# Layer 1 of the second and third chunk as seven block products, with weights streamed through a ring

## The reference

```python
interaction = jnp.einsum('bnd,bmd->bnm', bottom_output, bottom_output)
interaction_flat = interaction[:, _TRIL_R, _TRIL_C]
x = jnp.concatenate([bottom_mlp_output, interaction_flat, zero_pad], axis=1)
x = jax.nn.relu(x @ W0.T + b0)
x = jax.nn.relu(x @ W1.T + b1)
x = jax.nn.relu(x @ W2.T + b2)
x = jax.nn.relu(x @ W3.T + b3)
return x @ W4.T + b4
```

## Time and profile before

| | us |
|---|---|
| median of three runs (458.95 to 461.52) | 460.08 |
| the profiled execution, its own time | 456.55 |
| its span, first to last instruction | 454.7 |
| TensorE busy in the span | 443.1 |
| chunk two, from one layer 4 to the next (150.2 to 257.2) | 107.0 |
[...]

### The profile page before, as it was taken

One profiled execution on the slowest core, in us unless ns is written; L12 is line 12 of the kernel. 1 busy time (PEld: TensorE's weight loads), 2 busy tenths in 40 slices (PEclk: granted clock), 3 DMA queues, 4 the chain that ended last, 5 costly groups with the idle time before them and its releaser, 6 DMA issues.

```text
span 454.7 us, 12454 instructions
## 1 busy us (share of the span) xinstructions
PE 443.1 (97%) x5623; PEld 372.7 (82%) x5623; DVE 220.4 (48%) x414; ACT 136.9 (30%) x234; POOL 0.7 (0%) x6
## 2 busy tenths in 40 slices
PE   8998899999999999999999999999999999999995
PEld 7997888888888778888888788888788789999973
DVE  4876357343655452422325263324137878656343
ACT  4774333313332222111113222121113654422141
POOL 0000000000000000000000000000000000000000
PEclk9999999999999999999999999999999999999999
DMA  8999668463229325632671224723336120460100
GB/s 306 387 383 408 232 206 305 145 223 151 94 76 401 124 80 192 237 128 94 253 258 81 79 80 149 288 94 127 144 104 192 40 92 11 134 230 6 41 0 0
DMA packets 24102, 74.74 MB, mean 164 GB/s; under 512 B 2930, under 2 KB 9074, under 8 KB 20466
## 3 DMA queue, kind: packets, MB, share of 16 engines
q1 hardware_dynamic: 24050, 73.95, 45.3%
HBM read 65.55 MB, written 8.40 MB: 163 GB/s over the span
## 4 chain that ended last, share of the span: by engine, by line
PE 91%; DVE 4%; issue 2%; ACT 1%; DMA 1%; SPq 0%; DVEq 0%; ACTq 0%
PE work L1061 18%; PE work L1062 17%; PE work L1063 17%; PE acc L1061 8%; PE acc L1062 8%; PE acc L1063 8%; PE gps L1070 7%; PE acc L1088 2%; PE work L1088 1%; PE gps L1063 1%; PE gps L1062 1%; PE gps L1061 1%; DMA xfirst<-x_t 1%; PE gps L1111 1%; DVE turned L758 1%
## 5 line engine op out<-in xcount | busy, mean ns | idle before, releaser
L1061 PE MATMUL work<-h1h,w1s 128*128 128x512 f32 (+1 forms) x208 | 81.4, 391 | 0.0
L1063 PE MATMUL work<-h1l,w1s 128*128 128x512 f32 (+1 forms) x208 | 79.4, 382 | 0.0
L1062 PE MATMUL work<-h1h,w1s 128*128 128x512 f32 (+1 forms) x208 | 79.3, 381 | 0.0
L558 ACT ACTIVATE act_out<-work,bias 128x512 f32<-128x512 f32 (+1 forms) x56 | 36.7, 656 | 106.6 <-PE work L1063 105.0
L1063 PE MATMUL work<-featL,w0h 126*128 126x512 f32 (+5 forms) x160 | 55.4, 347 | 1.9 <-issue 1.9
L1062 PE MATMUL work<-featH,w0h 126*128 126x512 f32 (+5 forms) x160 | 55.9, 349 | 1.4 <-issue 1.4
L1061 PE MATMUL work<-featH,w0l 126*128 126x512 f32 (+5 forms) x160 | 57.1, 357 | 0.0
L1061 PE MATMUL acc<-h2h,w2l 128*128 128x512 f32 x128 | 51.0, 398 | 0.0
L796 DVE CAST h2h<-act_out 128x512 fp32r<-128x512 f32 x32 | 13.6, 426 | 75.7 <-ACT act_out L558 75.6
L1062 PE MATMUL acc<-h2h,w2h 128*128 128x512 f32 x128 | 49.9, 390 | 0.0
L1063 PE MATMUL acc<-h2l,w2h 128*128 128x512 f32 x128 | 49.8, 389 | 0.0
(11 more groups left out here) (127 smaller groups left out, 591.2 us busy)
## 6 DMA issues: line engine op xcount, KB each, us to landing
xraw<-x_t SPq DMA_DIRECT2D x48, 432.0 KB, 6.1
w1s<-w_parts SPq DMA_DIRECT2D x20, 1024.0 KB, 4.9
stage<-w_t SPq DMA_DIRECT2D x16, 512.0 KB, 5.9
w_parts<-w1s SPq DMA_DIRECT2D x8, 1024.0 KB, 4.9
xfirst<-x_t SPq DMA_DIRECT2D x9, 432.0 KB, 6.5
xmid<-x_t SPq DMA_DIRECT2D x5, 432.0 KB, 10.8
w0raw<-w_t SPq DMA_DIRECT2D x4, 512.0 KB, 10.5
w2raw<-w_t SPq DMA_DIRECT2D x4, 512.0 KB, 12.3
```

The costliest lines, as they stand in the source:

```text
L558: act.activation(act_out[:, slot(layer, m, more), cols], bank[:, cols], ACT.Relu, bias=bias[:, row:row + 1]).then_inc(relu_done, 1)
L1061: pe.matmul(dst, wl, ah, start=start, stop=False)
L1062: pe.matmul(dst, wh, ah, start=False, stop=False)
L1063: return pe.matmul(dst, wh, al, start=False, stop=stop)
```

## The change

- Chunks two and three do layer 1 in blocks too, as chunk four does; the gram units, pair picks and transposes for the next chunk are written by hand into the layers: units 0 and 1 behind layer-0 tiles 3 and 5, unit 2i + 2 behind P7 and unit 2i + 3 behind P3 of set i, the transposes of sub-batch i - 1 behind P6 of set i, the last ones ahead of the last layer-2 step. VectorE's picks of sub-batch i stand behind its two splits of set i.
- All S sums and their parts are made in chunk one, from the raw tiles in `stage` (which come in pairs i, 4 + i), and kept in device memory (`s_parts`, `keep_s`). `load_w1` waits for the sums of the pair before.
- Weights of the blocks come through `ring`, one place of 512 KB for each of the seven blocks, refilled when its block is done (`load_block`).
- Blocks and their sums use three banks; P1 and P5 are both copied out by ScalarE, U4 and C22 are made from the copy; C21 now stands ahead of C22, and both splits behind C12. The answers of the chunk before stand behind U2 of the first set.
- Gram units from chunk three's on use one bank, so each waits for the eviction of the one before. x has 4 slots.
- In chunk one layer 1 goes over its tiles in the order 0, 4, 1, 5, ..., and W2's parts follow that order.

```diff
-XSLOTS = 8
+XSLOTS = 4
...
-SUMS = ("U2", "U4", "C11", "U3", "C22", "C21", "C12")
+SUMS = ("U2", "U4", "C11", "U3", "C21", "C22", "C12")
...
+        def place(i, name):
+            banks = gps[:, 1, :], work[:, 0, :], work[:, 1, :]
+            return banks[(NB * i + BLOCKS.index(name)) % 3][:, 0:HALF]
...
+        UNIT_AT = {14: 1, 27: 2, 39: 3, 51: 4, 63: 5, 75: 6, 87: 7}
+        TURN_AT = {34: 0, 55: 1, 79: 2, 99: 3}
...
+        def unit_bank(g, u):
+            return gps[:, u % 2 if g == 1 else 0, :]
+        UNIT_BEHIND = {3: 0, 5: 1}
...
+        W2_AT = {33: 0, 46: 2, 77: 1, 90: 3}
+        W2_ORDER = list(W2_AT.values())
+        S_SUM_AT = {at + n: (i, n) for i, at in enumerate((20, 48, 73, 99)) for n in range(4)}
+        S_LO_AT = {at + 3 * n: (i, n) for i, at in enumerate((26, 54, 80, 105)) for n in range(2)}
...
             def load_w1(m):
                 if m >= 2:
                     sp.wait_ge(w1_done, m - 1)
-                sp.dma_start(stage[:, m % 2, :], w1[m, :, :]).then_inc(w_in[m % 2], 16)
+                    sp.wait_ge(s_sums, m // 2 * 4)
+                sp.dma_start(stage[:, m % 2, :], w1[L0_ORDER[m], :, :]).then_inc(w_in[m % 2], 16)
...
+            def keep_s(i):
+                sp.wait_ge(s_lo, 2 * i + 2)
+                for t, part in enumerate((sh, sl)):
+                    sp.dma_start(s_parts[i, :, :, t, :].rearrange("b p c -> p b c"),
+                                 part[:, i % 2, :, :].bitcast(f32)).then_inc(s_kept, 16)
+            def load_block(c, i, j):
+                    sp.wait_ge(block_done, nth_block(c, i - 1, BLOCKS[j]))
+                elif c > 1:
+                    sp.wait_ge(block_done, nth_block(c - 1, SETS - 1, BLOCKS[j]))
+                if c == 1:
+                    if (i, j) == (0, 0):
+                        sp.wait_ge(tile_done, nth(0, 1, MT1 - 1) + 1)
+                        for kept_slot in w1_kept:
+                            sp.wait_ge(kept_slot, kept(MT1 - 1))
+                        sp.wait_ge(s_sums, 4 * SETS)
+                    sp.wait_ge(s_kept, 32 * (i + 1))
+                name = BLOCKS[j]
+                if name in ("P1", "P2"):
+                    src = w1_parts[i, :, :, 0:WQ] if name == "P1" else w1_parts[i, :, :, WQ:]
+                elif name == "P4":
+                    src = w1_parts[SETS + i, :, :, WQ:]
+                    src = s_parts[i, ("P5", "P6", "P7", "P3").index(name), :, :, :]
+                sp.dma_start(ring[:, j, :, :].bitcast(f32), src).then_inc(ring_in[j], 16)
...
+            def first_body():
+                waits = {0: (2,), 1: (3,), 2: (5,), 3: (6,), 4: (7,), 5: (8,), 6: (9,), 7: ()}
+                stored = {1: 0, 3: 1, 5: 2, 7: 3}
+                for m in range(MT1):
+                    if m == 1:
+                        next_two(0, 3)
+                    if m == 2:
+                        next_two(0, 4)
+                    keep_w1(m)
+                    for u in waits[m] if m != 1 else ():
+                        next_two(0, u)
+                    if m + 2 < MT1:
+                        load_w1(m + 2)
+                    if m in stored:
+                        keep_s(stored[m])
+                load_x0(2)
+                for j in range(NB):
+                    load_block(1, 0, j)
...
+                    next_two(c, 2)
+                    next_two(c, 3)
+                for i in range(SETS):
+                    for j in range(NB):
+                        if i + 1 < SETS:
+                            load_block(c, i + 1, j)
+                        elif more:
+                            load_block(c + 1, 0, j)
+                        units = {(0, 4): 4, (0, 6): 5, (1, 4): 6, (1, 6): 7, (2, 4): 8, (2, 6): 9}
+                        if more and (i, j) in units and (units[(i, j)] < UNITS or later):
+                            next_two(c, units[(i, j)])
+                        if (i, j) == (1, 2):
+                            answer(c - 1)
+                            if later:
+                                load_x0(c + 2)
...
+            def block_out(c, i, name, dst):
+                act.wait_ge(block_done, nth_block(c, i, name))
+                ge(act, sum_done, nth_sum(c, i, name="C22") - NS if name == "P5" else nth_sum(c, i, "C11") - NS)
+                act.activation(dst, place(i, name), ACT.Copy).then_inc(copy_done, 1)
+            def relu_set(c, pos):
...
+            def layers(c, more):
+                for m in range(EARLY, MT0):
+                    relu(c, 0, m, work[:, m % 2, :])
+                    if m % 2 == 0:
+                        t1_hi_part(c, m // 2)
+                    elif m < MT0 - 1:
+                        others_hi_part(c, m // 2)
+                    if more and m in UNIT_BEHIND:
+                        grams_from_psum(c + 1, UNIT_BEHIND[m])
+                for i in range(SETS):
+                    block_out(c, i, "P1", P1_OUT)
+                    block_out(c, i, "P5", P5_OUT)
+                    if more and i:
+                        pairs_hi_part(c + 1, i - 1)
+                    if more and i < SETS - 1:
+                        grams_from_psum(c + 1, 2 * i + 2)
+                    relu_set(c, 2 * i)
+                    relu_set(c, 2 * i + 1)
+                    if more and i < SETS - 1:
+                        grams_from_psum(c + 1, 2 * i + 3)
+                if more:
+                    pairs_hi_part(c + 1, SETS - 1)
...
+                dst, block, part = {"U2": (U23, "P6", P1_OUT), "U4": (U4, None, P5_OUT), "C11": (first[:, left], "P2", P1_OUT),
+                                    "U3": (U23, "P7", U23), "C21": (second[:, left], "P4", U23),
+                                    "C22": (second[:, right], None, P5_OUT), "C12": (first[:, right], "P3", U4)}[name]
+                if block:
+                    dve.wait_ge(block_done, nth_block(c, i, block))
+                    dve.wait_ge(copy_done, 2 * (SETS * (c - 1) + i) + 2)
+                ge(dve, sum_done, nth_sum(c, i, name) - 1)
+                dve.tensor_tensor(dst, place(i, block) if block else U23, part, ALU.add).then_inc(sum_done, 1)
...
+            def layers(c, more):
+                for k in range(1, KQ):
+                    first_of_two(c, k)
+                    second_of_two(c, k)
+                for i in range(SETS):
+                    set_sum(c, i, "U2")
+                    if i == 0:
+                        answers(c - 1)
+                    set_sum(c, i, "U4")
+                    set_sum(c, i, "C11")
+                    if more and i:
+                        pairs_lo_part(c + 1, i - 1)
+                    set_sum(c, i, "U3")
+                    set_sum(c, i, "C21")
+                    set_sum(c, i, "C22")
+                    set_sum(c, i, "C12")
+                    split(c, 1, 2 * i, h2h[:, 0, :], h2l[:, 0, :])
+                    split(c, 1, 2 * i + 1, h2h[:, 1, :], h2l[:, 1, :])
+                    if more:
+                        if i == 0:
+                            dense_parts(c + 1)
+                        pair_picks(c + 1, i)
+                if more:
+                    pairs_lo_part(c + 1, SETS - 1)
...
-                pe.wait_ge(grams_out, SLICES * g + UNIT * (u - 1))
+                pe.wait_ge(grams_out, SLICES * g + UNIT * (u - (g == 1)))
...
+            def block(c, i, name, moving):
+                j = BLOCKS.index(name)
+                pe.wait_ge(ring_in[j], 16 * (SETS * (c - 1) + i + 1))
+                    cols = slice(k * P, (k + 1) * P)
+                    last = product(place(i, name), ring[:, j, 0, cols], ring[:, j, 1, cols], *moving(k), k == 0, k == KQ - 1)
...
+            def sets(c, more):
+                    p1(c, i)
+                    p5(c, i)
+                        layer2_blocked(c, 2 * i - 2)
+                    p6(c, i)
+                    if more and i:
+                        transpose_pairs(c + 1, i - 1, 2 * i + 2)
+                    p2(c, i)
+                        layer2_blocked(c, 2 * i - 1)
+                    p7(c, i)
+                    if more and i < SETS - 1:
+                        gram_unit(c + 1, 2 * i + 2, i)
+                    p4(c, i)
+                    p3(c, i)
+                    if more and i < SETS - 1:
+                        gram_unit(c + 1, 2 * i + 3, i)
+                layer2_blocked(c, KT2 - 3)
+                layer2_blocked(c, KT2 - 2)
+                if more:
+                    transpose_pairs(c + 1, SETS - 1, UNITS)
+                layer2_blocked(c, KT2 - 1)
...
+            def layers(c, more):
+                for m in range(EARLY, MT0):
+                    layer0(c, m)
+                    if m == EARLY:
+                        layer4(c - 1, True)
+                    if more and m in UNIT_BEHIND:
+                        gram_unit(c + 1, UNIT_BEHIND[m], 0)
+                sets(c, more)
```

More of the change, by code:

```diff
@@ L212, in first_slot @@
                 return xfirst[:, p, :]
[L213 to L218, removed]
+            if p < FIRST_LATE:
```

(31 more changed lines are left out.)

532 lines of the change are left out of this document (185 added, 347 removed).

## The result

The median after is 479.06 us (478.66 to 481.65, four runs) against 459.51 before on the same chip: a ratio of 1.0439 [1.0376, 1.0503]. The prediction was 457.2, its range ended at 461.8. The profiled execution took 478.72 us, its span is 476.9, 22.2 more than before.

What follows compares the result with a forecast made beforehand. TensorE was taken to bound the kernel. Products -6.7, chunk four's first set -1.0 and the fourth set's end +4.8 gave -2.9 us: 456.55 to 453.7, plus 3.5 for the runs' median, 457.2; range 452.8 to 461.8.

Steps and rivals of the forecast that it cites:

- Transfers ... Nothing: Reloading 14.7 MB for 8.4 in chunks two and three lands before the blocks want it, so it costs nothing.
- Chunk two, forecast at 106.1 us: Sign in the profile after: chunk two, between two layer-4 products, falls from 107.0 to about 106.1 us (-3.3 and +2.4).
- three signs that the prediction gave for being wrong: TensorE waits in every set (picks or ring), a block product takes 125 ns or more, or transposes find their pairs ready.
- A unit costs 1.40 us, before and after: nothing.: Each gram unit costs TensorE 1.40 us beyond the products around it; units only move, so no change in time.
- The idle stretch at 45.8: TensorE's 2.1 us idle in chunk one, read as of issue; used as that chunk's lower bound, -2.1 us.
- The clock: Rival, 6%: TensorE's clock falls in the 2.4 us waits at the end of set four in chunks two and three.
- The end of the fourth set: TensorE waits 2.4 us for the picks before the last transposes, once each in chunks two and three: +4.8 us.
- The products: In chunks two and three, 336 products of 256 columns replace 192 of 512 in each: 6.7 us saved for both.
- Chunk four's first set: Moving S work out and the answers behind U2 removes two waits for VectorE and slow starts: -1.0 us.
- Banks, picks of the first three sets: Three banks instead of four, and picks behind the splits in sets one to three, cause no TensorE wait: nothing.
- Chunk one: "0": The added S sums, roundings and activations in chunk one cost 0; bounds 2 us above and -2.1 below.
- x's fourth unit: Close place in chunk one: its load lands at 71.4 us, wanted by TensorE at 72.55, so it costs nothing.

## Why the prediction was wrong, step by step

- **"Transfers ... Nothing" is the step that failed.** It asked whether a refill lands before its block wants it, and that held: no block ever waited for the ring, a piece lands in 5.2 to 5.8 us. It did not ask whom the transfers delay. The loads of TensorE's own instructions cost 14.3 us in chunks two and three and 1.1 in chunk one. Chunk two, forecast at 106.1 us from one layer 4 to the next, took 122.3. None of the three signs that the prediction gave for being wrong names such a wait. The loads for matmuls 2866, 3244, 3622 and 4374 began 3.6 to 5.0 us after TensorE had passed the preceding boundary of 126 matmuls; in the later sets of chunk four the loads began 0.8 to 1.8 us before it.
- **"A unit costs 1.40 us, before and after: nothing."** As work this held, 1.39 with no wait in it. But where the waits stand, two stretches of 126 matmuls in a row now took 6.4, 7.8, 9.5 and 10.5 us without the waits in them; in chunks two and three of the kernel before no such pair took less than 10.9, since a 512-column product takes 0.227 us where one of 256 takes 0.12, and the units stood further apart. That is no limit, though: in its chunk one a pair took 8.1 us (from 55.3) without a wait. The price lay in where the units stand while the DMA engines are full.
- **The idle stretch at 45.8** was read as "of issue" and used as a bound for chunk one alone. It was a late instruction load (the table's second line). Together with the wait at 33.95, which the prediction did not mention, it was the sign in the trace before of what was to come:

```profile
35.69 0.28 PE L1062 MATMUL work<-featH,w0h 128*128 128x256 f32 x1 [1.35 <-issue]
```

  The rival that was missing is "more waits of this kind".
- **The clock.** The rival had 6 in 100. No run shows the price of a fallen clock that the range holds up to 461.8; it was the author's estimate. Measured were 1.3 to 1.7 us a fall, 2.3 for the long one. In the kernel after the clock fell five times in the work (at 48.3, 188.2, 215.5, 256.5 and 307.7 us), to 0.50 of full for 3.4 us (6.8 once), and the products in those stretches took 8 us more than at full clock. It fell behind the three longest waits; of those from 1.9 to 2.5 us it fell behind some (44.8 and 253.8) and not behind others (before's at 45.6, after's at 367.0). The prediction had one such case alone, the stretch at 45.8.
- **The end of the fourth set: right.** Forecast 2.4 us twice, measured 2.27 twice, and nothing took its place when it was removed. With the fall of the clock behind the first of them the step cost some 6 us, not 4.8.
- **The products: right in kind, 6.7 us forecast, 6.0 by the starts** (44.5 - 41.5, twice). 120 ns with th, tl and the ring held: the rows at 211 us are 0.12 apart. **Chunk four's first set:** the two waits are gone, 0.9 us (1.0 forecast); another 0.4 us went behind TensorE's last product, which was not forecast. **Banks, picks of the first three sets:** no wait, right.
- **Chunk one: "0", measured +1.9 us for x.** The close place that the prediction looked at, x's fourth unit, held by a hair: its landing was taken from the median, 6.1 us. It landed 1.8 us later than forecast, at 73.24, just in time for the unit at 73.33. The wait came at the fifth unit, 82.56, which the prediction did not look at. Its load stood behind 2 MB of S parts in the queue and took twice the median. The chain of waits of the kernel after:

```profile
69.22 1.88 SPq L396
71.10 0.04 issue
71.14 12.37 DMA xraw<-x_t
```

**The sum, redone:** instruction waits +15.4, clock +8, pairs +4.5, x +1.9, products -6.0, chunk four -1.3, the stretch ahead of matmul 851 -0.7 (before's own wait of 1.5 us at 33.95 is gone there, 0.7 us was lost elsewhere): +21.8 for the 22.2 of the spans. The 8 us of the clock are a reckoning from each matmul's usual spacing; the others are single places or differences of starts.

## What to carry to other kernels

Count an engine's instructions per microsecond, not only its busy time. Here TensorE ran out of instructions, for up to 3.7 us, where units of 256 in 1.4 us stood close together beside transfers of some 400 GB/s, and the profile showed that as an "issue" wait in the middle of an accumulation. Spread such bursts before streaming more through the DMA engines, and when pricing a transfer ask also whom it delays. A stretch without a releaser in the trace before is to be explained (here by the instruction queue's records) before it is set aside.

## What was unexpected of the hardware

- In the kernel after an instruction load took 0.9 to 1.7 us, and TensorE restarted 1.2 to 1.5 us after the end of the nine that it waited for. Beside other transfers at the three longest waits (398 to 411 GB/s, DMA share 1.01 to 1.03), a load that started late stopped TensorE for up to 3.7 us, at matmuls of the same series of 126 in every kernel with this order of work.
- Waits cost twice here: each fall of the clock, to 0.50, lasted 3.4 us (6.8 once) and cost 1.3 to 1.7 us (2.3 for the long one) on top of the wait ahead of it.
- A gain did not arrive in full: with the wait for x gone, the profiled execution kept 0.9 us of it up to 366 us and then lost 1.7 to a fall of the clock that after did not have there, behind the same wait for the pairs.
